# Scan of a two-layer kernel: another split between VectorE and GpSimd, the skip product in two halves, y copied earlier

## The reference, cut to what matters

```
half_dA   = 0.5 * delta[..., None] * A                  # A = -exp(A_log)
denom_inv = 1.0 / max(1.0 - half_dA, 1e-8)
A_bar     = (1.0 + half_dA) * denom_inv
Bx        = sqrt(delta) * B * denom_inv * xn
h_t       = A_bar_t * h_(t-1) + Bx_t                    # along the 2048 tokens
y_t       = sum over n of h_t[:, n] * C_t[n]
y         = y + D_skip * xn
```

## Time and profile before

| | us |
|---|---|
| median of three runs | 5092.32 (5089.25 to 5093.52) |
| profiled execution, whole | 5088.36 |
| its span | 5086.6 |
| DVE busy over the span | 4103.5 |
| POOL busy over the span | 1682.3 |
| scan of batch 0, about | 107 to 372 |
| scan of batch 1, about | 511 to 775 |
| scan of batch 2, about | 914 to 1178 |
| scan of batch 3, about | 1313 to 1578 |

### The profile page before, as it was taken

One profiled execution on the slowest core, in us unless ns is written; L12 is line 12 of the kernel. 1 busy time (PEld: TensorE's weight loads), 2 busy tenths in 40 slices (PEclk: granted clock), 3 DMA queues, 4 the chain that ended last, 5 costly groups with the idle time before them and its releaser, 6 DMA issues. The chain is left out here.

```text
span 5086.6 us, 90731 instructions
## 1 busy us (share of the span) xinstructions
PE 4492.6 (88%) x32649; PEld 2026.2 (40%) x32649; DVE 4103.5 (81%) x4837; ACT 3533.4 (69%) x6199; POOL 1682.3 (33%) x1155
## 2 busy tenths in 40 slices
PE   5778778777776699999899998999998999999998
PEld 3225225224223588888622222222222222222225
DVE  5997998898898332322399998999998999999996
ACT  5765766666663111111399998999998999999993
POOL 1883883883884322222211111021111211121003
PEclk8998998998998899999999999999999999999998
DMA  2402601201201655555311112121112211222016
GB/s 82 155 1 100 199 1 62 71 1 41 76 1 63 194 184 185 190 192 194 100 34 40 35 34 51 35 53 34 41 35 50 52 41 35 51 52 70 22 28 187
DMA packets 333697, 390.74 MB, mean 77 GB/s; under 512 B 172019, under 2 KB 288590, under 8 KB 322446
## 3 DMA queue, kind: packets, MB, share of 16 engines
q0 software_dynamic: 42784, 208.59, 12.6%
q1 hardware_dynamic: 286174, 174.18, 12.5%
q10 hardware_dynamic: 4352, 2.66, 0.2%
HBM read 248.78 MB, written 137.57 MB: 76 GB/s over the span
## 5 line engine op out<-in xcount | busy, mean ns | idle before, releaser
L1661 DVE TENSOR_REDUCE at_mpart<-at_ps 128x1 f32<-128x1024 f32 x2048 | 2348.1, 1211 | 87.8 <-PE at_ps L1550 55.5
L1646 ACT ACTIVATE at_E<-at_ps 128x512 f32<-128x512 f32 x4096 | 2222.3, 594 | 159.5 <-PE at_ps L1565 73.3
L1572 PE MATMUL at_ps<-at_E,at_vst 128*32 128x256 f32 x16400 | 1312.4, 391 | 24.7 <-ACT at_osb L1627 20.9
L1550 PE MATMUL at_ps<-at_ks,at_qs 48*128 48x512 f16 x4096 | 800.0, 387 | 51.8 <-DMA at_qs<-at_mrow 25.4
L1565 PE MATMUL at_ps<-at_qs,at_ks 50*128 50x512 f16 x4096 | 789.8, 382 | 21.6 <-ACT at_E L1646 20.7
L1434 POOL DMA_INDIRECT at_y<-yd,at_gidx x128 | 129.4, 1011 | 1662.5 <-DVE at_mx L1666 1581.0
L890 POOL TENSOR_TENSOR l_work<-l_work 128x1024 f32<-128x1024 f32 x256 | 604.3, 2361 | 78.7 <-DVE l_work L899 70.3
L1358 ACT ACTIVATE at_late<-at_ps 128x256 f32<-128x256 f32 x288 | 110.6, 384 | 638.9 <-PE at_ps L1301 638.9
L1572 PEld LDWEIGHTS at_ps<-at_E,at_vst 128*32 128x32 f32 x16400 | 326.4, 108 | 562.7 <-issue 412.5
L786 PE MATMUL l_ps<-l_bc,l_sel 96*128 96x512 bf16 x1024 | 313.3, 395 | 268.5 <-DVE l_work L899 126.7
L1550 PEld LDWEIGHTS at_ps<-at_ks,at_qs 48*128 48x128 f16 x4096 | 196.3, 92 | 870.3 <-DVE at_mpart L1661 451.5
(11 more groups left out here) (261 smaller groups left out, 4212.2 us busy)
## 6 DMA issues: line engine op xcount, KB each, us to landing
xd<-l_zero SPq DMA_DIRECT2D x4, 5120.0 KB, 33.7
yd<-l_zero SPq DMA_DIRECT2D x4, 5120.0 KB, 33.5
at_qs<-qp SPq DMA_DIRECT2D x132, 128.0 KB
at_ks<-kp SPq DMA_DIRECT2D x396, 32.0 KB
ot<-at_osb SPq DMA_DIRECT2D x516, 17.0 KB
at_qs<-qp SPq DMA_DIRECT2D x132, 64.0 KB
at_vst<-vp SPq DMA_DIRECT2D x65, 128.0 KB, 4.6
at_qs<-at_mrow SPq DMA_DIRECT2D x516, 2.0 KB
```

Of the source, the lines that this page charges most:

```text
L1550: mm = pe.matmul(ring[n % 2][:, r, :], m.qs[row, buf, bass.ts(i, P)], m.ks[row, buf, bass.ts(kh, BANK)], start=True, stop=True)
L1572: mm = pe.matmul(O[32 * q:32 * q + 32, :], m.vst[:, par, SLOTS_A * kk + sl, :], m.E[:, sl % 4, kk, bass.ts(q, QG)], start=(sl == 0 and kk ...
L1646: act.activation(m.E[:, sl % 4, kk, bass.ts(hf, BANK)], S[chunk(sl, 2 * hf + kk) % 3], ACT.Exp, scale=scale).then_inc(s.ex, 1)
L1661: dve.tensor_reduce(m.mpart[:, job:job + 1], ring[n % 2].rearrange("p a b -> p (a b)"), AX_X, ALU.max).then_inc(s.ring_free, 1)
```

## The change

Six edits in `scan_batch`:

- The split of B's weighing goes from column 512 to column 432. DVE weighs 432 columns, ACT copies 592 and POOL weighs 592.
- ACT copies B straight into the buffer of the weighed product, where POOL multiplies it by u in place. The buffer Bs is gone. The copy now waits for the product that last read that buffer (bx of unit i - 2) instead of POOL's first product.
- `weigh(i)` on DVE waits for ACT's copy of unit i (before: for PE's spread of B).
- The skip product no longer starts y. The first addition of a group does, and each half of the skip (one matmul) is added behind the addition of units 4 and 9 of the group.
- `y_out(i - 1)` stands at the end of ACT's iteration i = 16, 32, 48 and 64, one unit earlier than before.
- Unit 0: ACT makes inverse 0 and decay 0 first and copies no B for it; DVE weighs all 1024 columns and multiplies by inverse itself. POOL starts with unit 1.

```
-        LO, HI = slice(0, BANK), slice(BANK, HALF)
+        SPLIT, SKIP_AT = 432, (4, 9)
+        LO, HI = slice(0, SPLIT), slice(SPLIT, HALF)
...
                     if i:
                         pe.wait_ge(s.wa, i)
-                        pe.wait_ge(s.b_sbuf, i)
+                    if i >= 2:
+                        pe.wait_ge(s.b_sbuf, i - 1)
...
-                def skip(i):
+                def skip(i, q):
                     t0, k, n = unit(i)
-                    if i:
-                        pe.wait_ge(s.y_out, i // NS)
-                    for q in range(2):
-                        pe.matmul(y[:, q, :], m.dskip[:, k, :], m.xrT[:, k, t0 + BANK * q:t0 + BANK * (q + 1)],
-                                  start=True, stop=True)
+                    pe.matmul(y[:, q, :], m.dskip[:, k, :], m.xrT[:, k, t0 + BANK * q:t0 + BANK * (q + 1)],
+                              start=False, stop=True, skip_group_check=True)
...
-                    if i % NS == 0:
-                        skip(i)
+                    if i and i % NS == 0:
+                        pe.wait_ge(s.y_out, i // NS)
...
-                                       start=False, stop=True, skip_group_check=True)
+                                       start=(i % NS == 0), stop=True, skip_group_check=True)
                     mm.then_inc(s.y_added, 1)
+                    if i % NS in SKIP_AT:
+                        skip(i, SKIP_AT.index(i % NS))
...
                     if i >= 2:
-                        act.wait_ge(s.wb, i - 1)
-                    act.copy(Bs[i % 2], pB[:, 1, :]).then_inc(s.b_sbuf, 1)
+                        act.wait_ge(s.bx, i - 1)
+                    act.copy(w[i % 2][:, HI], flat(pB)[:, HI]).then_inc(s.b_sbuf, 1)
...
-                for i in range(2):
-                    b_out(i)
-                    inverse(i)
+                inverse(0)
+                decay(0)
+                b_out(1)
+                inverse(1)
                 for i in range(UNITS + 1):
-                    if i < UNITS:
+                    if 0 < i < UNITS:
                         decay(i)
...
-                    if i >= NS and i % NS == 1:
-                        y_out(i - 2)
-                y_out(UNITS - 1)
+                    if i and i % NS == 0:
+                        y_out(i - 1)
...
-                for i in range(UNITS):
+                for i in range(1, UNITS):
                     t0, k, n = unit(i)
-                    pool.wait_ge(s.b_sbuf, i + 1)
-                    if i >= 2:
-                        pool.wait_ge(s.bx, i - 1)
-                    pool.tensor_tensor(w[i % 2][:, HI], m.u[:, k, t0 + BANK:t0 + HALF], Bs[i % 2], ALU.mult).then_inc(s.wb, 1)
+                    pool.wait_ge(s.b_sbuf, i)
+                    pool.tensor_tensor(w[i % 2][:, HI], m.u[:, k, t0 + SPLIT:t0 + HALF], w[i % 2][:, HI], ALU.mult).then_inc(s.wb, 1)
...
-                    dve.wait_ge(s.b_psum, i + 1)
+                    dve.wait_ge(s.b_sbuf, i)
...
-                    dve.tensor_tensor(w[i % 2][:, LO], m.u[:, k, t0:t0 + BANK], pB[:, 0, :], ALU.mult).then_inc(s.wa, 1)
-
-                weigh(0)
+                    dve.tensor_tensor(w[i % 2][:, LO], m.u[:, k, t0:t0 + SPLIT], flat(pB)[:, LO], ALU.mult).then_inc(s.wa, 1)
+
+                dve.wait_ge(s.b_psum, 1)
+                dve.tensor_tensor(w[0], m.u[:, 0, 0:HALF], flat(pB), ALU.mult).then_inc(s.wa, 1)
+                dve.wait_ge(s.wa, 1)
+                dve.wait_ge(s.inv, 1)
+                dve.tensor_tensor(bx[0], w[0], inv[0], ALU.mult).then_inc(s.bx, 1)
                 weigh(1)
```

More of the change, by code:

```diff
@@ L753, in scan_batch @@
         inv, w, bx, h, hc = ([work(2 * n), work(2 * n + 1)] for n in range(5))
-        Bs = [m.work[:, 10 * HALF:10 * HALF + BANK], m.work[:, 10 * HALF + BANK:11 * HALF]]
         flat = lambda pair: pair[:].rearrange("p a b -> p (a b)")
         y, pC, pB, pdec = m.pair[0], m.pair[1], m.pair[2], m.pair[3]
-        LO, HI = slice(0, BANK), slice(BANK, HALF)
+        SPLIT, SKIP_AT = 432, (4, 9)
+        LO, HI = slice(0, SPLIT), slice(SPLIT, HALF)
         def unit(i):
@@ L872, in _ @@
                         inverse(i + 2)
-                    if i >= NS and i % NS == 1:
-                        y_out(i - 2)
-                y_out(UNITS - 1)
+                    if i and i % NS == 0:
+                        y_out(i - 1)
             @block.gpsimd
             def _(pool):
-                for i in range(UNITS):
+                for i in range(1, UNITS):
                     t0, k, n = unit(i)
-                    pool.wait_ge(s.b_sbuf, i + 1)
-                    if i >= 2:
-                        pool.wait_ge(s.bx, i - 1)
-                    pool.tensor_tensor(w[i % 2][:, HI], m.u[:, k, t0 + BANK:t0 + HALF], Bs[i % 2], ALU.mult).then_inc(s.wb, 1)
+                    pool.wait_ge(s.b_sbuf, i)
+                    pool.tensor_tensor(w[i % 2][:, HI], m.u[:, k, t0 + SPLIT:t0 + HALF], w[i % 2][:, HI], ALU.mult).then_inc(s.wb, 1)
                     pool.wait_ge(s.wa, i + 1)
-                    pool.wait_ge(s.wb, i + 1)
+                    pool.wait_ge(s.wb, i)
                     pool.wait_ge(s.inv, i + 1)
+                    if i == 1:
+                        pool.wait_ge(s.bx, 1)
                     if i >= 2:
```

## The result

| | before | after |
|---|---|---|
| median, us (4 runs each) | 5092.92 | 5053.81 (5050.66 to 5057.70) |
| ratio after to before | | 0.9924 (95% interval 0.9911 to 0.9936) |
| profiled execution, us | 5088.36 | 5054.9 |
| its span, us | 5086.6 | 5052.8 |

The change makes the kernel 39 us faster (33 to 45 by the interval). The forecast was 5054. To see where the time came from, I cut each batch's scan at four scan instructions. The first mark is the start of PE's first spread. Each entry is the difference of start times in the two traces; the last row is the sum over the four batches.

A forecast was written before the change was run, and what follows sets the result against it. DVE paced the scan at 3.91 and 3.97 us a unit, POOL close behind at 3.72. Savings of 8.1 us in four batches (32.4) plus 5.1 at starts gave 37.5, so 5054 from the 5092.32 median; range 5040 to 5074.

The forecast's parts named there:

- The bound passes from DVE to POOL: Ordinary units: POOL's period becomes 3.895 us, above DVE's 3.824 and 3.884; gain 0.015 then 0.075 us a unit.
- The text on what would show it: Signs in the profile after, among them scan to scan 3.89 us in both halves and POOL's products back to back.
- the 0.5 us by which scan 1 lags POOL: First half of a batch: 0.5 us taken off 30 x 3.895, giving 116.4 us after the change.
- The group boundary: Units 16, 32, 48: 5.2 us a batch goes; three stalls of 0.65 to 0.7 come, two stay, 1.3 us.
- The start: Batch start to scan 1: 1.0 us saved in batches 1 to 3, 2.1 in batch 0, 5.1 together.
- The skip halves and the copy behind POOL's product at nothing: Units 4 and 9, and ACT's copy of B: both cost 0; at worst 0.99 us a half, 0.1 a unit.
- No fall of TensorE's clock at the new boundary: Group boundaries: PE no longer waits for y behind an idle gap, so no clock fall is expected there.
- The sum: Scan 1 to 63: 3.2 plus 4.9 us saved a batch, 32.4 over four, plus 5.1 at starts: 37.5.
- the rival with DVE as the bound: All units: DVE stays the pace, 3.824 and 3.884 us; 5 us more saved, 5049, or 5041 without stalls; chance 0.09.
- the 122.0 beside it: Forecast's second half of a batch after the change: 31 x 3.895 + 1.3 = 122.0 us, without the last step.
- The rival that put 1.3 us on the clock: Three new boundaries: each costs 0.65 + 1.3 us as the stall moves and the clock falls; 5072; chance 0.12.

The follow-up runs named there:

- after_512: Changed kernel with the split back at column 512; ratio 0.9943 to the kernel before, sum of the scans 1018.4 us.
- after_384: Changed kernel with the split at column 384 instead of 432; ratio 0.9970 to the kernel before, sum of the scans 1023.9 us.
- y_after_decay: Changed kernel with y copied behind the decay and carry of the group's second unit; ratio 0.9919 to the kernel before, scans 997.5 us.
- after_noskip: Changed kernel with the skip product left out; ratio 0.9916 to the kernel before, sum of the scans 1001.7 us.
- before_again: The kernel before, unchanged, traced once more on another chip; one execution of 5091.36 us, sum of the scans 1045.2 us.
- boundary_only: Kernel before with only the earlier copy of y and the skip product in halves; ratio 0.9941 to the kernel before, scans 1023.2 us.

## Why the prediction was right

**The bound passes from DVE to POOL.** Right, in size too. POOL's period was given as 3.895 us and is 3.89; DVE's was given as 3.824 and is 3.83. after_512, 432 and after_384 bracket it: 1018.4, 1001.9, 1023.9 us. From 432 to 384 the period rises from 3.89 to 3.99 us, 48 columns at POOL's price. The text on what would show it said 3.89 in both halves; in the first half it is 3.83 for 6 to 13 units of a group and 3.89 for the rest. The sum had this in it, as the 0.5 us by which scan 1 lags POOL and as the stall that DVE catches up. In the second half the two periods (3.884 and 3.895 in the forecast) are too close for the steps of 3.89 to say which engine holds them.

**The group boundary.** Right in the sum: 5.2 us a batch gone, about 0.7 come three times, the first caught up. The new steps are 4.56, 4.57 and 4.65 us where the forecast was 0.65 to 0.7 over the period. y_after_decay shows the cause, since moving only the copy of y behind the decay removes them.

**The start.** Scan 1 is 2.0 and 0.9 us earlier (2.1 and 1.0 forecast). Scans 1 to 3 lose their stall in batches 1 to 3 (7.66 us for two steps); in batch 0 0.27 us of it stay.

**The skip halves and the copy behind POOL's product at nothing.** Right, by after_noskip and by the unchanged steps.

**No fall of TensorE's clock at the new boundary.** Wrong, and without cost: the 1.35 us that the addition then takes longer end 0.87 us before DVE needs the copy of B. That it is the missing skip passes that leave this room is argued, since no run has the skip at its old place with the earlier copy of y.

**The sum.** From scan 1 to 31 the four batches saved 13.6 us (12.8 forecast), from 31 to 62 19.8 (19.6), at the starts 4.7 (5.1): 38.1 in all against 37.5. That the median came within 0.2 us of the forecast is partly luck. The code outside the scans took 4 us more in one execution than in the other, and another execution of the kernel before has 5 us more in its scans. One figure of the prediction stands on another base than the rest: the 125.3 us of the rival with DVE as the bound count the short last step, which the 122.0 beside it leave out (121.7 without it). The 5 us that it draws from this are right.

**What the sum hid.** The working adds the parts as if each were worth its price alone. Alone they behaved otherwise. The start edit made the kernel a little slower, and of the split's 20 us a part came back at the old boundaries, whose passes on PE take 1.4 to 1.7 us longer over one fall of the clock. The rival that put 1.3 us on the clock had the size right and the place wrong: it sits in the kernel before. What selects the cheaper or the dearer form in a given batch stays open; before_again shows that it differs between two executions of the same code. The forecast needed only that the boundary be rebuilt together with the other edits, and it was. Counted from the first trace of the kernel before, 16.8 us are the boundary's, 4.8 those of the start and of the copy into the weighed buffer on top of it (after_512 against boundary_only), and 16.5 the split's on top of both. Against before_again the boundary's share is 22.0.

## What to carry to other kernels

Price a shift of work between two engines by both periods, each read where that engine waits for nothing: the busy share of POOL (33%) said nothing of an engine with 0.19 us left per unit. Before you spend such a gain, look for places where PE waits and then has several products in a row in the path, since their cost can jump with the granted clock (here four passes from 1.98 us to between 3.4 and 3.8 in the kernel before) and swallow a part of it. Here a few repeated matmuls in the wait removed the jump, and a boundary rebuilt so that PE had room hid it. Parts of a change are not always worth their price one by one, so a part that shows little alone may still be needed. And before you compare with a kernel whose time moves by itself, trace it more than once, and on the same chip.

## What the runs showed of the hardware

PE's matmuls at a boundary ran at either clock level (1.2 or 2.4 GHz) from one execution to the next with identical code: four f32 passes took 1.98 us or 3.43, and idle waits of 1.50 and 1.49 us stood before them. Repeating three spreads (1.3 us of work) so that the idle wait fell to 0.27 us kept the clock at its upper level at all twelve boundaries. GpSimd's f32 product costs 2.2 ns a column between 512 and 592 columns (1.266 and 1.442 us) and 2.1 up to 1024 (2.362 us); the one of 592 works in place, and no extra cost shows.
